# TensorE's order in two causal attentions: a list scheduler in the program instead of column counts and fixed bursts

## The reference

```python
# a: 16 heads of width 8, a rotary part of width 32 shared by all heads
c_kv = x @ W_kv_down
k, v, q = c_kv @ W_k_up, c_kv @ W_v_up, x @ W_q          # (B, T, 16, 8)
scores = einsum('bqhd,bkhd->bhqk', q, k) + einsum('bqr,bkr->bqk', q_rope, k_rope)[:, None]
w = softmax(where(causal, -inf, scores / sqrt(40)))
attn = einsum('bhqk,bkhd->bqhd', w, v) @ W_o
# b: the same with q, k, v from one product, scale sqrt(8), no rotary part
```

## Time and profile before

| | |
|---|---|
| median of 3 runs | 1206.3 us (1200.66 to 1209.1) |
| profiled execution | 1209.04 us, span 1207.3 us |
| PE busy | 1039.5 us, 86% |
| DVE busy | 594.8 us, 49% |
| ACT busy | 572.0 us, 47% |
| POOL busy | 241.9 us, 20% |
| mean granted TensorE clock | 0.93 of 2.4 GHz |

### The profile page before, as it was taken

How to read it: one execution, slowest core, us unless ns; L and a number is a source line. 1 busy time by engine, 2 the same in 40 slices (tenths; PEclk the granted TensorE clock), 3 DMA queues, 4 the chain that set the end, 5 groups by cost and what they waited for, 6 DMA issues and landing times. The chain is left out here.

```text
span 1207.3 us, 17627 instructions
## 1 busy us (share of the span) xinstructions
PE 1039.5 (86%) x6814; PEld 754.2 (62%) x6814; DVE 594.8 (49%) x1324; ACT 572.0 (47%) x1031; POOL 241.9 (20%) x488
## 2 busy tenths in 40 slices
PE   2724899999998799999985499999999859999998
PEld 0312555555654688899983255555555348889998
DVE  5624567777770744511124376766776174451111
ACT  1300456666666454444433046666666645444442
POOL 4010342344222100201007011222222210020000
PEclk9965899999999699999997679999999959999999
DMA  3333322321000400000002521211100040000001
GB/s 79 70 93 116 53 28 53 54 46 32 6 1 2 140 1 1 2 1 1 1 1 46 129 44 28 28 27 21 22 14 2 1 140 1 1 2 1 1 1 35
DMA packets 29916, 39.95 MB, mean 33 GB/s; under 512 B 4130, under 2 KB 22218, under 8 KB 29642
## 3 DMA queue, kind: packets, MB, share of 16 engines
q1 hardware_dynamic: 27610, 37.63, 14.7%
q10 hardware_dynamic: 2224, 1.20, 0.5%
HBM read 28.07 MB, written 10.49 MB: 32 GB/s over the span
## 5 line engine op out<-in xcount | busy, mean ns | idle before, releaser
L993 PEld LDWEIGHTS f_banks<-f_w,f_h 128*128 128x128 f32 x2048 | 241.1, 192 | 5.7
L993 PE MATMUL f_banks<-f_w,f_h 128*128 128x128 f32 x2048 | 243.4, 276 | 0.0
L1051 ACT ACTIVATE f_h<-f_banks,b_t 128x512 f32<-128x512 f32 x256 | 172.2, 688 | 144.2 <-PE f_banks L980 140.7
L980 PE MATMUL f_banks<-f_xr,f_w1r 128*128 128x512 f32 x768 | 199.7, 407 | 0.0
L762 DVE TENSOR_REDUCE a_mlate<-a_banks 128x2 f32<-128x1024 f32 (+3 forms) x120 | 124.8, 1079 | 81.3 <-PE a_banks L633 65.4
L980 PEld LDWEIGHTS f_banks<-f_xr,f_w1r 128*128 128x128 f32 x768 | 140.1, 193 | 25.0
L762 DVE TENSOR_REDUCE b_mlate<-b_banks 128x2 f32<-128x1024 f32 (+3 forms) x120 | 124.8, 1079 | 61.7 <-PE b_banks L633 46.4
L625 PE MATMUL a_banks<-a_k,a_q 120*128 120x512 f32 (+3 forms) x384 | 107.1, 384 | 45.2 <-POOL a_q L554 17.3
L1103 DVE SCALAR_TENSOR_TENSOR x<-f_banks,gate,x 128x128 f32<-128x128 f32 x160 | 45.1, 344 | 200.5 <-PE f_banks L993 200.5
L668 PE MATMUL a_banks<-a_q,a_k 121*128 121x512 f32 (+3 forms) x384 | 117.4, 388 | 11.0 <-DMA a_q<-a_mt 9.9
L668 PE MATMUL b_banks<-b_q,b_k 121*128 121x512 f32 (+3 forms) x384 | 116.3, 385 | 11.9 <-DMA b_q<-b_mt 10.2
(11 more groups left out here) (202 smaller groups left out, 1068.2 us busy)
## 6 DMA issues: line engine op xcount, KB each, us to landing
f_w<-in_w SPq DMA_DIRECT2D x32, 256.0 KB, 5.6
a_k<-scratch_k SPq DMA_DIRECT2D x24, 128.0 KB
a_q<-scratch_q SPq DMA_DIRECT2D x24, 128.0 KB
b_k<-scratch_kb SPq DMA_DIRECT2D x24, 128.0 KB
b_q<-scratch_q SPq DMA_DIRECT2D x24, 128.0 KB
a_k<-scratch_r SPq DMA_DIRECT2D x18, 128.0 KB
a_q<-scratch_r SPq DMA_DIRECT2D x18, 128.0 KB
scratch_kb<-b_k_hl SPq DMA_DIRECT2D x16, 128.0 KB, 2.8
```

What stands on the lines that cost most here:

```text
L980: last = pe.matmul(h_ps[:, j, :], w1r[e % 2][wp][:, j * P:(j + 1) * P], xr[xp][:, chunk(c)], start=(i == 0), stop=(i == 2))
L993: last = pe.matmul(y_ps[:, q % 2, i * P:(i + 1) * P], h[q % 2][:, j, i * P:(i + 1) * P], w2[:, e, j, :], start=(j == 0), stop=(j == HB - 1))
L1051: act.activation(h[q % 2][:, j, :], h_ps[:, j, :], ACT.Gelu, bias=m.b1_t[:, e * HB + j:e * HB + j + 1]).then_inc(gelu_done, 1)
```

## The change

`beside_table`, `piece_order`, `ring_table`, `BURST`, `COPY_O` and `TURN_O` go. In their place a class `Plan` keeps four clocks (PE, DVE, ACT, POOL) with fixed costs per instruction, and `planned()` builds PE's order step by step: it takes the item that can start first; items that can start by PE's present time plus 50 ns count as equal, and go in the order piece or turn of maxima, output turn, values, score. The table `AFTER[u]` says what PE does behind score unit u, and `COPIES` where ACT copies an output. DVE follows the same table. One table serves both attentions. `LEAD`, the pieces and their order, the ring's two slots, the score banks and the buffers are as before. No instruction is added or removed; POOL's and SP's programs are untouched.

```diff
+class Plan:
+    COLUMN, LOAD, ENTER, LEAVE, SEEN, BACK = 0.44, 115, 155, 112, 260, 150
+    def matmul(self, ready, columns):
+        at = max(self.pe + (self.LEAVE if self.in_values else 0), self.pe_start + self.LOAD, ready)
+        self.pe_start, self.pe, self.in_values = at, at + columns * self.COLUMN, False
+        return self.pe + self.SEEN
+    def four_heads(self, ready, columns):
+        at = max(self.pe if self.in_values else max(self.pe + self.ENTER, self.pe_start + self.LOAD), ready)
+        self.pe_start, self.pe, self.in_values = at, at + 3.64 * columns * self.COLUMN, True
+        return self.pe + self.SEEN
+    def slot_free(self):
+        return self.ring[-2] + self.BACK if len(self.ring) >= 2 else 0.0
+    def reduce(self, seen, lengths):
+        self.dve = max(self.dve, seen) + sum(160 + 1.045 * n for n in lengths) + 20
+        self.ring.append(self.dve)
...
+    def turn(self, j):
+        self.reduce(self.matmul(self.turn_ready(j), P), [30])
+        self.m_there[j] = self.dve + 2400
+    def score(self, i, v):
...
+        begin = max(self.act, seen, self.valued[at - NPT] if v % GH == 0 and at >= NPT else 0.0)
+        self.exped.append(begin + 170 + 0.84 * columns)
+        self.act = self.exped[-1] + 25
+        if 4 * c <= SETS[c][s][0]:
+            self.pool = max(self.pool, self.exped[-1] + 60) + (410 if len(SETS[c][s]) == 2 else 290)
+            self.masked[i, s] = self.pool
+    def values_ready(self, i, s):
...
+        return max(self.exped[last], self.masked.get((i, s), 0.0), copied) + self.BACK
...
+def planned():
+    while units or sets or o < len(HALVES):
+        choice = []
+        if ring:
+            if ring[0][0] == "turn":
+                choice.append((plan.turn_ready(ring[0][1]), 0, ring[0]))
+            elif issued < scored + LEAD:
+                choice.append((plan.slot_free(), 0, ring[0]))
+        if o < len(plan.copied):
+            choice.append((plan.o_ready(o), 1, ("o", o)))
+        if sets and plan.values_ready(*sets[0][1:]) is not None:
+            full = units and SET0[units[0][1]] + units[0][2] // GH >= len(plan.valued) + NPT
+            choice.append((plan.values_ready(*sets[0][1:]), -1 if full else 2, sets[0]))
+        if units and SET0[units[0][1]] + units[0][2] // GH < len(plan.valued) + NPT:
+            if plan.score_ready(u) is not None:
+                choice.append((plan.score_ready(u), 3, units[0]))
+        key = min(choice, key=lambda c: (max(c[0], plan.pe + 50), c[1]))[2]
...
-        pieces(-1)
+        beside(-1)
         for i, (n, c) in enumerate(HALVES):
             for v in range(NU[i]):
                 score_unit(i, v)
-                pieces(UNIT0[i] + v)
-                if v % GH == GH - 1:
-                    for s in BURST[c][v // GH]:
...
-                if v == TURN_O and i:
-                    turn_o(i - 1)
+                beside(UNIT0[i] + v)
```

More of the change, by code:

```diff
@@ L108, in beside_table @@
[L108 to L125, removed]
@@ new lines, in planned @@
+def planned():
+    ring = [("piece", j, x) for j, (n, c) in enumerate(HALVES) for x in range(len(PIECES[c]))]
+    for j, (n, c) in enumerate(HALVES):
+        last = ring.index(("piece", j, len(PIECES[c]) - 1))
+        ring.insert(min(last + 1 + TURN_AFTER, len(ring)), ("turn", j))
+    units = [("score", i, v) for i, (n, c) in enumerate(HALVES) for v in range(NU[i])]
+    sets = [("values", i, s) for i, (n, c) in enumerate(HALVES) for s in range(len(SETS[c]))]
+    plan, after, copies = Plan(), {-1: []}, {}
+    issued = scored = u = o = 0
+    while units or sets or o < len(HALVES):
[14 more added lines that the diff above has]
+        key = min(choice, key=lambda c: (max(c[0], plan.pe + 50), c[1]))[2]
+        if key[0] == "score":
+            plan.score(*key[1:])
+            scored += set_tiles(HALVES[key[1]][1], key[2] // GH)[1]
+            after[u] = []
+            u += 1
+            units.pop(0)
+            continue
+        after[u - 1].append(key)
+        if key[0] == "piece":
+            plan.piece(*key[1:])
+            issued += 2 * CH
+            ring.pop(0)
+        elif key[0] == "turn":
+            plan.turn(key[1])
+            ring.pop(0)
+        elif key[0] == "o":
+            plan.turn_o(o)
+            o += 1
+        else:
+            plan.values(*key[1:])
+            sets.pop(0)
+            if len(plan.copied) > len(copies):
+                copies[len(copies)] = u - 1
+    return after, copies
@@ L130 @@
+AFTER, COPIES = planned()
+RING = {}
+for keys in AFTER.values():
+    for key in keys:
+        if key[0] != "values":
+            RING[key] = len(RING)
 KEEP = 3
@@ L740, in scalar @@
                                scale=scale).then_inc(exp_done, 1)
-                if v == COPY_O and i:
-                    copy_o(i - 1)
-        copy_o(NH2 - 1)
+                for done, unit in COPIES.items():
+                    if unit == u:
+                        copy_o(done)
     def vector(dve):
@@ L789, in normalise @@
                               ALU.mult).then_inc(ring_done, 1)
-        def pieces(u):
-            for j, x in BESIDE[u]:
-                if (j, x) == TURN[j]:
-                    copy_m(j)
-                else:
+        for u in range(-1, UNIT0[-1]):
+            for key in AFTER[u]:
+                if key[0] == "piece":
+                    j, x = key[1:]
                     take_max(j, x)
@@ L798, in pieces @@
                         join(j)
-        pieces(-1)
-        for i in range(NH2):
-            for v in range(NU[i]):
-                pieces(UNIT0[i] + v)
-                if v == TURN_O and i:
-                    normalise(i - 1)
-        normalise(NH2 - 1)
+                elif key[0] == "turn":
+                    copy_m(*key[1:])
+                elif key[0] == "o":
+                    normalise(*key[1:])
     stage = Stage()
```

103 lines of the change are left out of this document (62 added, 41 removed).

## The result

The changed kernel took 1230.5 us (median of 4 runs, 1228.3 to 1234.1), the kernel before 1207.7 us beside it (4 runs, 1200.7 to 1216.6): a ratio of 1.0188, 95% interval 1.0115 to 1.0261. The change costs about 23 us by the medians (14 to 31 us by the interval) and 19.3 us by the spans of the two profiled executions. The forecast was 1220 us with a range of 1203 to 1236: the sign held and the time lies in the range, but the loss that was forecast, 12 us over 1207.7, is little more than half of the measured one.

A forecast was written before the change was run, and what follows sets the result against it. PE was taken as the bound in the long middle of each attention. From the profiled 1209.0 us, −7 + 11.5 + 4 + 2 + 3 + 0 gave 1222.5; with the median 2.7 us lower, the forecast was 1220 us, range 1203 to 1236.

The forecast's parts named there:

- both middles, without casts: Long middles of both attentions: four added bursts cost 1.6 us, removed stalls save 2.1 us a group; −7 us, bounds −28 to +24.
- start of a: Start of attention a: PE stands before first values until the masks, with 6 pieces behind; +11.5 us, bounds −3 and +16.
- late masks in a: Halves (2,1), (3,1), (4,1) of attention a: values wait on masks behind casts; 6 us less 2 already paid, +4 us.
- start of b: Start of attention b: PE stands before the fourth score until about 696.9, turn at about 712.5; +2 us (−2 to +5).
- maxima rows: Later-started halves (n,1): row takes about 3.7 us, plan says 2.4; 0.2 us of stall each, +3 us (0 to +18).
- tails: End of each attention: single sets hold ACT up half as long, twice as often; 0 us (−6 to +3).
- I take all of it, 0 to 2.1: Middle groups: all three PE waits on DVE go, saving 2.1 us a group, bounds 0 to 2.1.
- about 0.4 us: Middle groups: what a burst of values costs PE beyond its columns; four more bursts a group, 1.6 us.
- the stalls only move: Rival for the middle: rows late at every half, or pieces still meet a busy slot; +15, 1235 to 1240 us, chance 0.16.
- again less 2.4 us of work no longer left: Start of attention b: credit against the later turn, 712.5 not 708.06, for work already done; 2.4 us.
- bursts pair up: Rival for the middle: only one or two bursts added, −1.3 us a group, −17 in all; about 1210 us, chance 0.30.
- The starts are not hit: Rival for the starts: first values behind group 0's last piece, PE fills the idle 17 us; 1192 us, chance 0.12.

The follow-up runs named there:

- experiment 3: Changed kernel, with POOL's wait on loads and spreading of rotary rows for groups 3 and up moved behind the half's masks; 1226.5 us, 1.0117 of the kernel before.
- experiment 5: Changed kernel, its plan taking 3.7 us instead of 2.4 us for the maxima row to arrive; 1227.7 us, 1.0134 of the kernel before.
- experiment 7: Order of the kernel before up to the first score of half (7,1), new planner only for the last two halves; 1208.1 us, 0.9989 of the kernel before.
- experiment 2: Changed kernel, its plan told that attention a's first half is masked no earlier than 24.5 us from its zero; 1223.2 us, 1.0088 of the kernel before.
- experiment 6: Order of the kernel before up to the first score of half (1,1), new planner from there; 1217.5 us, 1.0062 of the kernel before.
- experiment 1: Kernel before, with values of every set by itself, ten bursts a group instead of six; 1219.6 us, 1.0063 of the kernel before.
- experiment 9: Old starts, paired sets, 3.7 us row and casts in the plan, plus faster ACT and dearer burst changes in the plan; 1198.3 us, 0.9899 of before.
- experiment 8: Changed kernel with old order for the starts, paired sets, 3.7 us for the maxima row and a's casts in the plan; 1197.1 us, 0.9889 of before.
- experiment 10: New planner throughout with paired sets, no old order, its plan told of late ACT, POOL, group 1's pieces, maxima rows and casts; 1196.3 us, 0.9884 of before.
- experiment 4: Changed kernel, with values in the middle offered only when two sets are ready; 1224.9 us, 1.0100 of the kernel before.
- the informed plan: New planner throughout, told of the other engines' late starts, the maxima rows and casts; 1196.3 us with paired sets, 1202.4 us with single sets.

## Why the prediction came out as it did

Each term of the sum, against the two traces:

| term | predicted | measured | from |
|---|---|---|---|
| both middles, without casts | −7 | +3.4 | b +1.7; a taken as the same |
| start of a | +11.5 | +11.5 | 75.7 to 88.6, less the 1.4 of the first turn |
| late masks in a | +4 | +4.4 | 6.1 − 1.7; experiment 3: 3.8 |
| start of b | +2 | +4.6 | 58.6 to 63.2 |
| maxima rows | +3 | in the middles | 0.25 of wait a group; experiment 5 didn't take it away |
| tails | 0 | −5.2 | nearly half of it moved work, by experiment 7 |

**The start of a was right in its mechanism up to the turn; that the sum fits exactly is luck.** The first values stand behind 12 pieces and 6 scores (I had 7); PE waits until 125.93 (I had 126.8), the turn comes at 138.21 (139.8), the second half's scores at 143.03 (144.5). Experiment 2 takes two thirds of the cost away and experiment 6 all of it, each by another edit, so it is shown and not only argued. The 9.09 us of idle have no releaser in the record, but PE's next product comes 0.1 us after POOL's fourth mask, and the six pieces behind it, which need no mask, run only then. The Trainium skill says the same (TensorE: Matmul & The Clock Gate, "Step-by-step: what each phase is for"): matmuls stay in program order and only weight loads go ahead. This trace agrees: 9.09 us at one product and 6.24 us at another, with ready work behind each.

Two errors cancel. Up to the second half's first score the loss is 9.2 us (143.03 less 133.81), where I had 10.7. Behind it the loss is 2.3 us, where I had 0.8: some 3.2 for late casts less 2.4 of work already done. Of the casts only a wait of 0.96 us is in the record (the values at 164.36; it names ACT, but POOL's masks end at 164.21), and the idle time of this part is the same as before. What grew is the busy time, with 10.1 us at half the clock, for which my sum has no term: the granted clock was at its upper level from 129.2 to 139.2 and fell again from 139.4 to 149.5.

**The middle was wrong, and it is the step that failed**: "I take all of it, 0 to 2.1" and "about 0.4 us" a burst. Both sizes were off, against each other. The burst is 0.23 us by experiment 1, so four cost 0.9 and not 1.6. Setting the starts of the same products in before and in experiment 1 side by side, an added burst costs 0.08 us on entering, 0.11 on leaving and 0.06 at the product behind, on average, and everything else gives back 0.02. I had 0.17, 0.15 and 0.09, because I held the gaps against the shortest one, 0.24 us; where no burst stands, the same scores are followed after 0.12 to 0.32 us. The stalls: the three on DVE were worth 0.76 + 0.58 + 0.50 = 1.84 us a group, and they did go. The rest follows by difference: a group takes 33.33 against 33.03, so the new order adds 0.30 − 0.92 + 1.84 = 1.2 us a group of its own. In the record stand new waits of 0.22 and 0.17 us on ACT and 0.25 on the row, 0.64 us together; the other 0.6 us is in the busy time and isn't itemised. I had "the stalls only move" as a rival, at 0.16; it belonged into the forecast. Why the freed time is spent isn't settled: experiment 9 mends ACT's cost in the plan and doesn't gain, and experiment 5 left the wait on the row as it was.

**The start of b was too small by 2.6 us.** The turn was right: 712.5 forecast for a start as early as before, 727.28 less the shift of the first turn, 15.5, measured: 711.8. What failed is the credit "again less 2.4 us of work no longer left". From the second half's turn to its first score pass 4.8 us in after (727.28 to 732.10) and 4.7 before, where this row of PE's timeline is that score:

```profile
712.79 0.50 PE L668 MATMUL b_banks<-b_q,b_k 121*128 121x512 f32 x1 [0.58 <-ACT b_k_hl L739]
```

After has no work left to fill that way and idles 2.28 us before it, where before idled 0.58. From that score to the end of the start it takes 24.6 us in after and 23.8 before, with less idle time (0.4 against 1.2 us) but 4.5 us of it at the lower clock, where before there were none. So the work done ahead saved nothing. One trace of a start is good to 1 or 2 us: with the same order at the start, experiments 2 and 3 have 61.3 and 64.4 us in b.

**The casts** were right in size, in part by luck. I counted waits alone, 6 us less 2 already paid. Against the middle of b, that of a has 2.3 us more added idle time and 2.1 us more added busy time (from the table by stages). Two stretches of 3.4 us at half the clock stand in it, and the sum has no term for them. Experiment 8 shows that the plan, when told of them, finds an order in which they cost nothing: its groups of a are 32.4 us there, less than the 33.3 to 34.4 of before.

**The tails** gained 5.2 us by my marks. I gave them 0 with −6 to +3. By experiment 7 at most 1.3 us of each is a real gain, the rest was done ahead.

Of the rivals, "bursts pair up" didn't happen (ten bursts a group, as forecast). "The starts are not hit" is wrong. "The stalls only move" is nearest to what happened, with about 1.2 us a group or 14 us over the twelve groups, of which my sum held 3 as maxima rows. It came otherwise than I had it, though: no piece meets a busy slot any more, and the time stands in waits on ACT and the row and in busy time. Cheaper bursts (0.7 us a group, 8 us) and the tails hid most of it in the total.

From 1220 to 1230.5: middles +10.4, start b +2.6, casts +0.4, start a 0, rows −3, tails −5.2, together +5.2; some 0.6 outside the marks; and 4.9 because I took the median 2.7 us below the profiled execution, where it lies 2.2 above (1230.5 and 1228.3). Rounding takes 0.2 off.

**What stays open.** In experiment 10 the long first group of a is put down to group 2's loads from its two waits only; an edit that tells the plan of them wasn't tried, nor was the old start in a joined to the informed start in b. By their stages (a's start and middle 271.6 and 274.6 us in experiments 8 and 10, b's 254.7 and 250.0) that would be 4.7 us under experiment 8, if the parts add. What the wait on the maxima row is worth, and why pairing gives back only half of what experiment 1's price promises, is open too. What limits a group of b at 32.6 us with pairs isn't known either; PE's busy share there is 98% (192.06 of 195 us in experiment 4, by busy time in the stretch 760 to 955).

## What to carry to other kernels

An order made from a plan is as good as the waits that the plan knows: on an engine that runs in order, one item placed ahead of its operand costs everything behind it (9.1 us at one product here), and moving it behind the other ready work took 8.2 us of the 12.9 at that start away (experiment 2). A wait can also cost more than its length: behind most waits of some 2 us the clock was at its lower level for 3.4 us. So compare a plan with the trace stage by stage, first at the starts and where other engines serve loads, and put the late starts of the other engines into it. And let the plan change between kinds of work less often: the informed plan gained 8 us with single sets and 14 with pairs.

## What the runs showed of the hardware

- Changing from full-array products to a burst of four-head values and back cost 0.23 us of PE's time beyond the columns in the order of before (experiment 1: four more bursts, 33.03 to 33.96 us a group), less than the 0.4 us that the starts of the neighbours seem to add up to. It shows as busy time, not as idle time. In the new order five bursts fewer gave back less (experiment 4: 3.5 us of busy time over 29 bursts in the middle of b).
- A stall's idle time in the record is less than its cost: 0.52, 0.41 and 0.39 us of idle are 0.76, 0.58 and 0.50 us by start times, since the modelled ends of the matmuls overlap what follows.
- Behind a wait of PE of about 2 us in the middle of a, the granted clock was often 0.50 for 3.4 us: after waits of 2.08 and 2.22 us in after, 1.78, 2.05 and 2.31 in experiment 6, 2.32 and 2.65 in experiment 2. Not always: waits of 2.12 us in experiment 2 and 2.03 in experiment 5 had no such stretch behind them, and of three waits of 1.26 or 1.27 us in experiment 3 one had. A group with a wait of 2.12 us and the full clock took 35.6 us, those with waits of 2.08 and 2.22 us and the lower clock 36.8 and 36.9.
- A shorter start did not need a higher mean clock. The start of b has a mean granted clock of 0.77 before (678.0 to 736.6), the same in after (693.3 to 756.5), and 0.79 in experiment 10, whose row is below, though it is 4.4 us shorter than before and 9.1 shorter than after. PE's idle time in it is 14.1, 18.4 and 7.7 us:

```profile
674.10:728.30 54.20, 46.49 (x243) 28.34 (x244) 36.17 (x43) 20.85 (x40) 7.15 (x22) 0.79 0.32 68
```
